# Inverse norms by logarithm and exponential, b2 inside w2, and an interleaved distance setup in a four-layer transformer kernel

## The reference, cut to what matters

```python
# distance attention, Q = x @ W_k.T by heads
sq = sum(Q * Q, axis=-1);  dist = sq - 2 * (Q @ Q.T) + sq.T
attn = softmax(-dist / sqrt(8));  out = attn @ Q, then merged and W_o

# local pass: two layers of this, windows of 64 with the one before
h = shift_token(x);  q, k, v = split(h @ wqkv)          # 8 heads of 64
q = q / clip(norm(q), 1e-12) * q_scale;  k likewise
q, k = rotary_xpos(q, k);  x = x + softmax(8 * q @ k.T + mask) @ v @ wo
h = layernorm(shift_token(x)) * lg + lb
a, g = split(h @ w1 + b1);  x = x + (a * gelu(g)) @ w2 + b2   # 341 hidden channels
```

## Time and profile before

| | |
|---|---|
| median of 3 runs | 3577.19 us (3571.36 to 3577.69) |
| profiled execution | 3580.72 us, span 3578.6 us |
| granted TensorE clock, mean | 0.959 |
| PE busy | 3183.2 us, 89% |
| ACT busy | 2167.5 us, 61% |
| DVE busy | 1976.4 us, 55% |
| POOL busy | 1737.4 us, 49% |
| distance attention with its setup | about 87 to 650 us |
| first local pass | about 755 to 1540 us |
| second local pass | about 2779 to 3567 us |

### The profile page before, as it was taken

How to read it: one execution, slowest core, us unless ns; L and a number is a source line. 1 busy time by engine, 2 the same in 40 slices (tenths; PEclk the granted TensorE clock), 3 DMA queues, 4 the chain that set the end, 5 groups by cost and what they waited for, 6 DMA issues and landing times. The chain is left out here.

```text
span 3578.6 us, 73165 instructions
## 1 busy us (share of the span) xinstructions
PE 3183.2 (89%) x26564; PEld 1951.8 (55%) x26564; DVE 1976.4 (55%) x4014; ACT 2167.5 (61%) x3580; POOL 1737.4 (49%) x1412
## 2 busy tenths in 40 slices
PE   6499999868999999749999999999998599999995
PEld 5222222435666666526666666666665366666663
DVE  4200000337777777545556555656565577777773
ACT  2399999526666666535555555555554366666663
POOL 1100000039889988523333333333332698998882
PEclk9699999979999999979999999999999799999998
DMA  1122222021111111100000000000000211111111
GB/s 33 20 36 39 36 38 38 7 74 34 35 36 38 37 36 34 25 10 9 7 6 9 6 9 6 9 6 9 6 6 4 86 37 35 37 37 37 35 33 36
DMA packets 124405, 95.70 MB, mean 27 GB/s; under 512 B 80448, under 2 KB 100544, under 8 KB 123968
## 3 DMA queue, kind: packets, MB, share of 16 engines
q1 hardware_dynamic: 122784, 89.41, 11.4%
q10 hardware_dynamic: 1440, 3.80, 0.3%
HBM read 22.90 MB, written 2.10 MB: 7 GB/s over the span
## 5 line engine op out<-in xcount | busy, mean ns | idle before, releaser
L1761 POOL TENSOR_SCALAR e<-e,inv 128x768 f32<-128x768 f32 (+7 forms) x512 | 375.3, 746 | 761.8 <-DVE inv L1653 761.8
L1724 ACT ACTIVATE e<-e,nmax 128x768 f32<-128x768 f32 (+7 forms) x512 | 395.4, 772 | 429.5 <-DVE e L1648 426.2
L1648 DVE TENSOR_SCALAR_CACHE_REDUCE e<-slot 128x768 f32<-128x768 f32 (+7 forms) x512 | 376.2, 754 | 243.8 <-PE slot L1537 243.8
L530 ACT ACTIVATE e<-slot 128x1024 f32<-128x1024 f32 x512 | 472.9, 1091 | 43.8 <-PE slot L466 43.8
L896 POOL TENSOR_TENSOR inv_norm<-floored,minus_half 128x16 f32<-128x16 f32 x128 | 374.1, 2922 | 10.7
L1641 DVE COPY eT<-slot 128x512 f32<-128x512 f32 (+3 forms) x384 | 238.7, 622 | 234.1 <-PE slot L1548 233.9
L1548 PE MATMUL slot<-ident,e 128*128 128x128 f32 x2304 | 332.7, 280 | 8.7 <-POOL e L1761 3.7
L1531 PE MATMUL slot<-key,q 64*128 64x512 f32 (+3 forms) x1536 | 318.1, 518 | 19.0 <-ACT v L1711 12.7
L889 POOL TENSOR_TENSOR rot<-cosine,sine 128x1024 f32<-128x1024 f32 x128 | 302.1, 2360 | 44.3 <-DVE sine L1228 44.3
L857 POOL TENSOR_TENSOR prob<-prob,inv_total 128x1024 f32<-128x1024 f32 x128 | 242.6, 1895 | 129.2 <-DVE inv_total L1246 129.2
L1548 PEld LDWEIGHTS slot<-ident,e 128*128 128x128 f32 x2304 | 252.5, 141 | 92.0 <-issue 68.9
(11 more groups left out here) (161 smaller groups left out, 6420.8 us busy)
## 6 DMA issues: line engine op xcount, KB each, us to landing
v_mix<-v SPq DMA_DIRECT2D x256, 128.0 KB, 2.3
w_qkv<-in_causal_w_dram SPq DMA_DIRECT2D x32, 192.0 KB
query<-q_hi SPq DMA_DIRECT2D x128, 32.0 KB
keys<-q_hi SPq DMA_DIRECT2D x128, 32.0 KB
query<-q_lo SPq DMA_DIRECT2D x128, 32.0 KB
keys<-q_lo SPq DMA_DIRECT2D x128, 32.0 KB
hs<-H SPq DMA_DIRECT2D x32, 128.0 KB
h1s<-H SPq DMA_DIRECT2D x32, 128.0 KB
```

The lines of the kernel that those rows point to most:

```text
L530: act.activation(e[n % E_RING][:], c.slots[n % RING][:].rearrange(flat), ACT.Exp, scale=2 * SCALE).then_inc(e_ready, 1)
L1648: dve.tensor_scalar(e[n % RING][h][:, 0:cols], c.slots[h][:].rearrange(flat)[:, 0:cols], -1.0, None, ALU.mult, ALU.min, accum_out=nmax[:, ...
L1724: act.activation(part, part, ACT.Exp, bias=nmax[:, n, h:h + 1], scale=-1.0, accum_out=total[:, n, h:h + 1]).then_inc(e_ready, 1)
L1761: pool.tensor_scalar(part, part, inv[:, n, h:h + 1], 1.0, ALU.mult, ALU.mult).then_inc(scaled, 1)
```

## The change

Three parts. (1) In the local pass the power on POOL is replaced: ACT takes the logarithm of the floored squared norms and the exponential of minus half of it (Ln and Exp from one table set), and POOL refines it by one Newton step of four small operations, one tick later, ahead of the unit rows. The first operations of ACT stand between `turned_out` and `exp`. (2) b2 is put into a free row of w2: the first padded hidden channel gets the constant biases 0.0625 and 16, so that gate times value is 1; POOL's addition goes, and with it the load of b2. (3) In the distance setup the separate block of `normalised_columns` goes; normalising, transposes, copies and products of all batches interleave in one block, and SP issues the 40 stacking transfers of the first unit in that block (`stack_head`) instead of after the barrier.

```diff
+                def inverse_norms(a):
+                    first = first_inv[:, a.j % 2, :]
+                    pool.wait_ge(first_inv_ready, a.t + 1)
...
+                    pool.tensor_tensor(inv_square[:], first, first, ALU.mult).then_inc(inv_square_ready, 1)
...
+                    pool.tensor_tensor(product[:], inv_square[:], floored[:, a.j % 2, :], ALU.mult).then_inc(correction_ready, 1)
...
+                    pool.sem_inc(correction_seen, 1)
+                    pool.tensor_scalar(correction[:], product[:], -0.5, 1.5, ALU.mult, ALU.add).then_inc(correction_ready, 1)
...
+                    pool.tensor_tensor(inv_norm[:, a.j % 2, :], correction[:], first, ALU.mult).then_inc(inv_norm_ready, 1)
...
-                def add_b2(a):
-                    pool.wait_ge(h1s_loaded, 80 * a.g + 80)
-                    rows = H[:, bass.ds(row(a.g), G), :]
-                    pool.tensor_tensor(rows, rows, b2[a.depth][:].unsqueeze(1).broadcast_to([P, G, P]), ALU.add)\
-                        .then_inc(b2_ready, 1)
...
-                    pool.tensor_tensor(inv_norm[:], floored[:], minus_half[:].broadcast_to([P, 2 * HEADS]), ALU.pow)\
-                        .then_inc(inv_norm_ready, 1)
...
                         if turned := tile(step, r, PT, depth):
                             scale(turned)
                         if last := tile(step, r, 1, depth):
+                            inverse_norms(last)
                             unit_rows(last)
                         if r == 1 and (ffn := group(step, FFN, depth)):
                             deviations(ffn)
-                            add_b2(ffn)
                         if own := tile(step, r, 0, depth):
                             rotated(own)
-                            inverse_norms(own)
+                            floor_norms(own)
...
+                def inverse_norms(a):
+                    act.wait_ge(floor_ready, 3 * a.t + 3)
+                    act.activation(log_norm2[:], floored[:, a.j % 2, :], ACT.Ln).then_inc(log_norm2_ready, 1)
+                    act.wait_ge(log_norm2_ready, a.t + 1)
...
+                    act.activation(first_inv[:, a.j % 2, :], log_norm2[:], ACT.Exp, scale=-0.5).then_inc(first_inv_ready, 1)
...
-                            act.preload_act_table(ACT.Exp)
+                            act.preload_act_table_set("natural_log_exp_and_others")
...
                         if turned:
                             turned_out(turned)
+                        if own:
+                            inverse_norms(own)
                         if scored:
                             exp(scored)
...
                     dve.wait_ge(down_ready, a.g + 1)
-                    dve.wait_ge(b2_ready, a.g + 1)
...
+    bias[:, 0, hid], bias[:, 1, hid] = 0.0625, 16.0
     down = np.zeros((n, chunks * P, P), w2.dtype)
-    down[:, :hid] = w2
+    down[:, :hid], down[:, hid] = w2, b2
```

In the first fence `inverse_norms` stands twice, first POOL's, then ACT's. The setup follows; SP's part moves 4, 4 and 2 transfers a head, the loop over batches is PE's (behind two groups of transposes), and the last lines are DVE's, behind the first eight tiles:

```diff
-            normalised_columns(nc, c, xT, moments=False)
+            row_statistics(nc, c, moments=False)
...
+                @block.sync
+                def _(sp):
+                    heads = [stack_head(sp, stacked, 0, 0, j) for j in range(GROUP)]
+                    sp.wait_ge(cleared, 5)
+                    sp.wait_ge(hi_ready, 1)
+                    for high, _, _ in heads:
+                        high()
+                    sp.wait_ge(lo_ready, 1)
+                    for _, low, _ in heads:
+                        low()
+                    sp.wait_ge(norm_hi_ready, 1)
+                    sp.wait_ge(norm_lo_ready, 1)
+                    for _, _, norms in heads:
+                        norms()
...
+                    for b in range(B):
+                        columns(b)
+                        if b < B - 1:
+                            turn_rows(2 * b + 2)
+                            turn_rows(2 * b + 3)
+                        rows(b)
+                        norms(b)
...
+                        if b < B - 1:
+                            rows(2 * b + 2)
+                            rows(2 * b + 3)
                         dve.wait_ge(hi_ready, b + 1)
                         dve.wait_ge(sq_ready, b + 1)
                         dve.tensor_tensor(q_lo[:, cols], c.slots[1][:].rearrange(flat), q_hi[:, cols].bitcast(F32),
                                           ALU.subtract).then_inc(lo_ready, 1)
...
+                        dve.wait_ge(norm_hi_ready, b + 1)
+                        dve.tensor_tensor(n_hl[32:32 + HEADS, cols], c.slots[2][0:HEADS].rearrange(flat),
+                                          n_hl[0:HEADS, cols].bitcast(F32), ALU.subtract).then_inc(norm_lo_ready, 1)
```

More of the change, by code:

```diff
@@ L316, in _, with turn_rows, columns @@
                 def _(pe):
[L317 to L326, removed]
-                            m = pe.matmul(c.slots[2][0:HEADS, half, :], sel[:], sq[b % 2][:, half * 512:half * 512 + 512],
-                                          start=True, stop=True)
-                        m.then_inc(norm_ready, 1)
[L331 to L337, removed]
+                    def turn_rows(i):
+                        pe.wait_ge(xn_ready, G * (i + 1))
+                        if i >= 2:
+                            pe.wait_ge(columns_ready, i - 1)
+                        for j in range(G):
+                            m = pe.transpose(c.slots[3][:, i % 2, j * P:(j + 1) * P], xn[:, i % 2, j, :], c.ident[:])
+                        m.then_inc(turned, 1)
+                    def columns(b):
+                        pe.wait_ge(columns_ready, 2 * b + 2)
                         if b:
@@ L344, in _, with rows @@
                         m.then_inc(qT_ready, 1)
-                        if b == 0:
-                            pe.wait_ge(merged_ready, 1)
[L347 to L350, removed]
+                    def rows(b):
+                        if b:
+                            pe.wait_ge(q_out, b)
+                        for t in range(TPB):
+                            m = pe.matmul(c.slots[0][:, t // 4, (t % 4) * P:(t % 4 + 1) * P],
+                                          xT[:, (b * TPB + t) * P:(b * TPB + t + 1) * P], wk[:], start=True, stop=True)
+                        m.then_inc(q_ready, 1)
@@ new lines, in norms @@
+                    def norms(b):
+                        pe.wait_ge(sq_ready, b + 1)
+                        if b:
+                            pe.wait_ge(norm_hi_ready, b)
+                            pe.wait_ge(norm_lo_ready, b)
+                        else:
+                            pe.wait_ge(merged_ready, 1)
+                            pe.wait_ge(eff_out, 1)
+                        for half in range(2):
+                            m = pe.matmul(c.slots[2][0:HEADS, half, :], sel[:], sq[b % 2][:, half * 512:half * 512 + 512],
+                                          start=True, stop=True)
+                        m.then_inc(norm_ready, 1)
@@ L352, in _, with columns @@
                 @block.scalar
                 def _(act):
[L354 to L357, removed]
+                    def columns(i):
+                        act.wait_ge(turned, i + 1)
+                        act.activation(xT[:, i * G * P:(i + 1) * G * P], c.slots[3][:, i % 2, :], ACT.Copy).then_inc(columns_ready, 1)
@@ L359, in _ @@
+                    columns(0)
+                    columns(1)
                     for b in range(B):
-                        act.wait_ge(q_ready, b + 1)
-                        act.activation(q_all[:, b * TPB:(b + 1) * TPB, :, :].rearrange("p t h d -> p (t h d)"),
-                                       c.slots[0][:].rearrange(flat), ACT.Copy).then_inc(q_out, 1)
                         act.wait_ge(qT_ready, b + 1)
@@ L670, in local_layers @@
         small = [sb(f"small{l}", [P, 8]) for l in range(DEPTH)]
-        b2 = [sb(f"b2{l}", [P, P]) for l in range(DEPTH)]
         scales = [sb(f"scales{l}", [P, 2, 2, D]) for l in range(DEPTH)]
@@ L1206, in _ @@
                 columns(group(0, 0, None))
[L1207 removed]
+                act.preload_act_table_set("natural_log_exp_and_others")
                 for l in range(DEPTH):
[L1209 removed]
+                    act.wait_ge(w_out_loaded[l], 64)
                 over_steps(act, ticks)
```

133 lines of the change are left out of this document (91 added, 42 removed).

## The result

The changed kernel takes 3685.03 us (median of 4 runs, 3682.16 to 3690.01), the kernel before, with one more run beside it, 3576.22 us (3571.36 to 3577.69). The ratio is 1.0308 [1.0290, 1.0326]: slower by 109 us. The profiled execution took 3690.0 us, its span is 3688.2 us at a mean granted clock of 0.949.

A forecast was written before the change was run, and what follows sets the result against it. It took a chain of waits alternating between PE and POOL as the bound, neither alone. Local passes +142, filling -4 and setup -31 made +107 on 3580.7, so 3688; the median 3.5 lower, 3684 us (3610 to 3760).

The forecast's parts named there:

- The ring: Local passes: scale, POOL's floor, ACT's pair, exponential, DVE's totals and next scale wait in a circle; step 49.15 us against 44.1.
- Rival 1: Local passes: floor early enough to hide ACT's pair, POOL's relief decides, PE bounds; 3472 us, chance 0.10.
- The terms: Scale-to-scale times of local-pass ticks: 10.89 us (r=0), 12.78 (r=1), 14.21 (r=2), 11.27 (r=3).
- The mis-sized term: Local-pass tick r=2, with Gelu table load, gates and DVE's products before the totals: 14.21 us, the largest term.
- The load of the table: Gelu table load in tick r=2: 1.28 us, gate starting 1.30 after it, without the skill's further drain.
- The filling path, -4: Ahead of each local pass's first scale, two or three powers become cheaper: -2 us a pass, -4 in all.
- b2 as a row: Feed-forward of the local pass: PE +0, POOL's addition of 1.28 us goes, counted within tick r=1.
- The setup: Distance setup: interleaved batches and first stack transfers hidden beside them, first score at 135.3, 32 earlier; -31 us.
- The ring of batches: Distance setup: DVE normalises the next eight tiles only behind norm_low, so batches 1 and 2 take 8.96 us each.
- Rival 2: Local passes come out even with today's ticks and only the distance setup counts; 3546 us, chance 0.06.
- rival 3: Local passes slow as forecast, but distance setup gives nothing, a stack or norm_low wait replacing it; 3715 us, chance 0.05.
- Rival 4: ACT's tables reload between logarithm and exponential, two loads of 1.28 us a tick; 3996 us, chance 0.03.

The follow-up runs named there:

- the floor ahead of the sum: The changed kernel with POOL's floor of the norms issued before the rotated sum; 3556.5 us, ratio 0.9953.
- power kept: The kernel before with the new distance setup and b2 in w2, the power still on POOL; 3499.6 us, ratio 0.9787.
- norms alone: The changed kernel with the old distance setup and POOL's addition of b2 restored; 3758.9 us, ratio 1.0515.
- b2 alone: The kernel before with b2 in w2, power and distance setup as before; 3529.8 us, ratio 0.9875.
- the two runs of one part alone: The kernel before with only the new distance setup, 3548.8 us; the changed kernel with the old distance setup, 3720.6 us.
- Newton in its own tick: The changed kernel with POOL's order scale, unit rows, floor, rotated sum, deviations, then the refining operations of the tick's own tile; 3498.9 us, ratio 0.9781.

## Why the prediction was right

It said 3684 (3610 to 3760), slower with 0.82, by a ring round which POOL's floor, ACT's pair, the exponential, DVE's totals and POOL's scale go. Measured 3685.0. Point by point:

- **The ring.** Shown by its own waits (237.5 us before the logarithm, 515.2 before the scale), by the tick taken apart above, and by experiment: exchanging two of POOL's lines gives back 128 us, another order of the same operations all of it. Rival 1 (POOL's relief decides) is out for this kernel. It named the point from which it would hold, the floor out about 2.2 us sooner; the floor ahead of the sum is 2.36 sooner, and then an ordinary tick (r=0) is 10.5 us, as with the power kept.
- **The terms**, in the second pass. r=0: 10.89 foreseen, 10.82 to 11.00 measured; r=1: 12.78, 12.7 to 13.1; r=3: 11.27, 11.15 to 11.2. r=2: 14.21, and 14.14 in every other step only. First six ticks: 10.89, 10.82. In the first pass r=0 reaches 11.28 and seven of the fourteen r=2 ticks are 14.1.
- **The mis-sized term** is r=2 in the steps between, 14.8 to 15.0 (14.4 to 15.0 in the first pass). In either kind of tick PE starts its products after 4.67 us of idle time and at half its clock, and in the long one it stays there longer (two products at L1040 end 2.08 us after they begin, 1.80 in the short one, at the full clock 1.02). So probT's copy ends late and the logarithm starts behind it, 8.41 us after the scale of 3487.60 and without a wait (7.73 in the tick taken apart). Here the ring goes through PE, which the forecast held to be of no account. That makes 745.95 us between the first scale (2866.31) and the 62nd (3612.26), where 742.5 was forecast: +74.3 for +70.8. In the first pass it is +72.4 (743.85 for 671.44).
- **The load of the table** costs what the earlier trace rows show: 1.28 us, the gates 1.30 behind its start. The drain that the Trainium skill states ("ScalarE: Activation LUTs", "What ACT_TABLE_LOAD costs") is not there; with it each of the 28 such ticks would be 1.38 us longer.
- **The filling path, -4.** From the start of a pass (POOL's clear of `edge`) to its first scale it is 53.26 and 53.45 us before, 52.66 and 52.09 after: -2.0 together. The sums for the passes, +148.0 where the forecast had +138, are then +146.7 between the scales, -2.0 ahead of them and +3.3 behind the 62nd (the causal attention with it), where the forecast had nothing.
- **b2 as a row.** The term was right (1.25 off r=1; 13.92 with the norms alone, 12.7 in the changed kernel). What the prediction didn't say is how much it brings without the ring: 44.5 us. "POOL's relief" was treated as one thing, and its small part was the one on the path.
- **The setup.** Forecast -31; the first exponential is 30.3 us earlier. The ring of batches is 8.8 us (norms at 107.70, 116.49, 125.28; 8.96 foreseen). That is the best case: in seven of the eight other traces of the new setup one or both take 10.1 to 10.4. The first score itself is at 136.50, 1.2 later than the 135.3 forecast: DVE's first tiles took 4.16 us for 2.14 beside the memsets, which the forecast had costed at nothing. SP issued the first stack from 105.56 to 132.3, forecast from 101.6; it stayed hidden, but by less. The total up to the local pass is -38.4 in this pair of profiles. Of it 7.8 us lie behind the first exponential, and they belong to the two profiled executions rather than to the change: from the first exponential to the last the distance attention takes 487.3 us before and 479.5 after, and about 482 (481.9 to 482.2) in the three other profiles with the old setup, 482.3 to 483.1 in seven of the eight with the new one (487.2 in the eighth). Before's excess is in its first unit, where the granted clock is 0.50 from 168 to 183; the kernel with b2 alone has 0.50 from 168 to 173 and 1.00 from 178 on. In the medians the setup is -25.5, -30.2 (power kept against b2 alone) and -35.6.

The right total of 3684 is thus in part luck: passes 10 us dearer, and the part ahead of them 7 us cheaper than forecast.

Rival 2 (the local passes even) and rival 3 (setup gives nothing) are out by the two runs of one part alone. Rival 4 (tables loaded anew) is out: the whole kernel has 76 table loads as before, 32 of them at L1297 as at L1201, and none stands within a pair.

## What to carry to other kernels

Before a small operation is put into an engine's queue, ask what stands behind it and when its input is ready in the tick: an operation of 0.22 us that waits for the last thing another engine does can cost 5 us a step, while the engine it relieves gets emptier. Order on the producing side comes first: put what another engine waits for ahead of long work that nobody waits for, and check whom the displaced long work then keeps waiting. And test the parts of a joint change singly: here two brought 75 us together and the third took 185.

## What was not expected of the hardware

- **PE's clock falls behind the gap.** The steps shown of before and of the kernels with the power kept and with Newton in its own tick have a granted clock of 1.00. In the changed kernel, where PE is idle for 4.67 us ahead of r=2, the clock falls to its lower level for part of that tick, 3.4 us and 5.6 us by turns in the second pass (an estimate from the means of 0.88 in 14.1 us and 0.81 in 14.8). Why the two lengths alternate stays open. A long gap is not needed: before has the clock at 0.50 to 0.67 from 3440 to 3444 in its own second pass, behind idle times of 1.53 and 0.50 us, and that tick of r=2 is 11.2 us long where most are 10.0.
- **POOL's memset and DVE's fp32 tensor_scalar disturb each other.** Eight tiles of 128x128 take 2.14 us alone and 4.16 beside memsets, the memsets of 128x1024 1.09 to 1.10 for 0.95. The Trainium skill ("SBUF — State Buffer", "SBUF: two separate sides") calls the pair of ports that the two share an exclusive lock, held for the whole instruction by a GpSimd operation or by a DVE operation in a 2-port mode or, against a GpSimd operation that reads SBUF, with two inputs in SBUF, the loser fully blocked. That they disturb each other agrees; in which mode DVE was, no trace here shows. As full exclusion for the whole duration of each it doesn't agree: from 95.15 to 99.35 eight tiles and four memsets were done, 4.2 us, where one after the other they need 2.14 + 3.8 = 5.9.
- **A power of few elements is dear in proportion.** On POOL the power of 128x16 takes 2.92 us and that of 128x4 1.04, so by an estimate 0.16 us for each element more in a partition; a multiplication of 128x16 takes 0.22.
